# Depthwise convolution of a transformer block's feed-forward part: one run of 32x32 array tiles over four banks in place of two runs of 64x64 tiles

## The reference, cut to what matters

```python
def bit_linear(x, w):                 # values: round(x * 127 / max|x| per row), weights: -1, 0, 1 and a scale
    return jnp.einsum('bsd,hd->bsh', xq, wq)

h = bit_linear(x, w1)                 # 16 x 128 x 256 -> 16 x 128 x 1024
h = depthwise_conv1d(h.transpose(0, 2, 1), conv_w, conv_b)   # 3 taps along the 128 rows, each of the 1024 units by itself
h = jax.nn.silu(h.transpose(0, 2, 1))
return bit_linear(h, w2)              # -> 16 x 128 x 256
```

## Time and profile before

| what | value |
|---|---|
| runs | 995.89, 996.27, 1000.37 us; median 996.27 us |
| profiled execution, first to last instruction (its span) | 992.7 us |
| its mean granted TensorE clock | 0.962 of 2.4 GHz |
| PE busy over the span | 891.3 us (90%) |
| feed-forward part | about 876 to 992.7 us of the span |
| PE instructions of CV in the trace | 1536 matmul records, 1536 weight loads |

### The profile page before, as it was taken

One profiled execution on the slowest core, in us unless ns is written; L12 is line 12 of the kernel. 1 busy time (PEld: TensorE's weight loads), 2 busy tenths in 40 slices (PEclk: granted clock), 3 DMA queues, 4 the chain that ended last, 5 costly groups with the idle time before them and its releaser, 6 DMA issues. The chain is left out here.

```text
span 992.7 us, 26217 instructions
## 1 busy us (share of the span) xinstructions
PE 891.3 (90%) x8784; PEld 758.1 (76%) x8785; DVE 612.0 (62%) x1561; ACT 469.1 (47%) x1209; POOL 379.8 (38%) x555
## 2 busy tenths in 40 slices
PE   4888889777999999997999899999999999779995
PEld 3677667636999999995556598888888887667784
DVE  3588788754455555542017466768667686549895
ACT  3777777712222222221333444445444454349895
POOL 4477677530000000006101446445464444426762
PEclk9998999987999999998999999999999999879998
DMA  4454447432433333315765798897989986411121
GB/s 119 145 164 145 143 148 237 140 145 94 128 108 93 98 93 108 93 44 181 262 225 180 165 188 185 179 182 164 200 172 176 172 178 150 90 33 55 60 61 49
DMA packets 222059, 137.78 MB, mean 139 GB/s; under 512 B 160289, under 2 KB 207393, under 8 KB 221857
## 3 DMA queue, kind: packets, MB, share of 16 engines
q1 hardware_dynamic: 180304, 99.78, 40.1%
q10 hardware_dynamic: 38608, 28.64, 10.8%
q0 software_dynamic: 3072, 8.39, 2.6%
HBM read 81.79 MB, written 54.98 MB: 138 GB/s over the span
## 5 line engine op out<-in xcount | busy, mean ns | idle before, releaser
L1717 ACT ACTIVATE c_pT<-c_T 128x512 f32<-128x512 f32 (+2 forms) x90 | 50.2, 595 | 104.4 <-PE c_T L1876 73.3
L1666 POOL TENSOR_TENSOR c_soft<-c_soft,c_share 128x616 f32<-128x616 f32 (+2 forms) x96 | 70.3, 760 | 63.4 <-DVE c_share L2129 61.8
L1062 ACT ACTIVATE b_rowsT<-b_RT 128x256 f32<-128x256 f32 x39 | 15.0, 383 | 158.2 <-PE b_RT L1104 158.2
L1173 DVE COPY b_w<-moe_w 128x1024 f32 x78 | 53.5, 687 | 56.2 <-issue 50.7
L1676 POOL MEMSET d_round<- 128x1 f32 x1 | 0.1, 98 | 226.5 <-POOLq L953 226.5
L1113 PEld LDWEIGHTS b_G<-b_rowsT,b_w 128*128 128x128 f32 x624 | 77.2, 195 | 4.2 <-DVE b_w L1173 1.5
L1113 PE MATMUL b_G<-b_rowsT,b_w 128*128 128x128 f32 x624 | 77.9, 279 | 1.5 <-ACT b_rowsT L1062 1.3
L1113 PE MATMUL b_U<-b_rowsT,b_w 128*128 128x128 f32 x624 | 76.1, 275 | 0.0
L1187 DVE SCALAR_TENSOR_TENSOR b_hidT<-b_U,b_bias,b_gate 128x128 f32<-128x128 f32 x156 | 43.9, 343 | 51.9 <-PE b_U L1113 45.4
L1140 PE MATMUL b_Y<-moe_w,b_hidT 128*128 x312 | 73.9, 380 | 0.9 <-DVE b_out L1218 0.9
L1113 PEld LDWEIGHTS b_U<-b_rowsT,b_w 128*128 128x128 f32 x624 | 72.9, 192 | 0.0
(11 more groups left out here) (231 smaller groups left out, 2167.2 us busy)
## 6 DMA issues: line engine op xcount, KB each, us to landing
rel_windows<-c_relw ACTq DMA_DIRECT2D x28, 368.0 KB, 6.7
c_bias<-rel_windows SPq DMA_DIRECT2D x16, 616.0 KB, 5.6
prob_rows<-c_soft SPq DMA_DIRECT2D x16, 616.0 KB, 7.3
moe_w<-in_L_Wl SPq DMA_DIRECT2D x16, 512.0 KB, 4.1
early<-in_L_early SPq DMA_DIRECT2D x16, 384.0 KB, 3.2
values<-c_pT ACTq DMA_DIRECT2D x22, 256.0 KB, 3.8
b_rows<-expert_lists SPq DMA_DIRECT2D x39, 128.0 KB, 2.0
expert_out<-b_out SPq DMA_DIRECT2D x39, 128.0 KB, 1.7
```

The source lines that it names most:

```text
L1173: nc.vector.tensor_copy(own[p][h][:, :, :], w1[:, bass.ds(e, 1), :, h * HE:(h + 1) * HE].rearrange("p o c n -> p (o c) n"))\
L1666: ins = nc.gpsimd.tensor_tensor(soft[p][:, hs, a:z], soft[p][:, hs, a:z], share[:, s, hs].unsqueeze(2).to_broadcast([P, HS, z - a]), ALU.mult)
L1717: nc.scalar.activation(dst, view(T[k]), ACT.Copy, **kw).then_inc(g["emptied"], 1)
```

## The change

The 16 blocks' work of a batch becomes one run, `convolve(b, p)`: 96 matmuls, each on one 32x32 tile. Blocks 0 to 3 go with the first three taps' turns, blocks 4 to 7 with the second; for each tap 16 matmuls follow each other on the 16 tiles. Row quarter `a` of the array writes to bank `CV[a]`, block `m` = half * 4 + turn puts its quarter `a` into quarter (a + turn) % 4 of the output's partitions, and the host permutes the second weight matrix and the biases to suit (`turned_quarters`). The run waits once, for `d_hp`(b+1) and for all eight SiLUs of the batch before, and raises `cv_mm` once; all eight SiLUs of a batch wait for that. The list of PE loses its second call. POOL's tap matrices are 128x32 in place of 128x64.

```diff
-    c["halves"] = np.concatenate([np.eye(P // 2, dtype=np.float32)] * 2)
+    c["quarters"] = np.concatenate([np.eye(P // 4, dtype=np.float32)] * 4)
...
-                    nc.gpsimd.tensor_scalar(shared["tap"][:, m, k, :], cst("halves"), taps[:, m, k:k + 1], None, ALU.mult)
+                    nc.gpsimd.tensor_scalar(shared["tap"][:, m, k, :], cst("quarters"), taps[:, m, k:k + 1], None, ALU.mult)
...
         def tiles_of(half):
-            return [(half * 2 + u + cross * MH // 2, cross, CV[half * 2 + cross][:, u * P:(u + 1) * P]) for u in two for cross in two]
+            return [(half * 4 + r, CV[r][:, half * P:(half + 1) * P]) for r in range(4)]
...
-                act.wait_ge(g["cv_mm"], 2 * b + half + 1)
+                act.wait_ge(g["cv_mm"], b + 1)
                 since(act, g["rounded"], b - 1)
-                for m, _, region in tiles_of(half):
+                for m, region in tiles_of(half):
...
-            def convolve(b, p, half):
-
-                if half == 0:
-                    pe.wait_ge(g["h"], b + 1)
-                apart(pe, g["silu"], 2 * (b - 1) + half + 1)
-                tiles = tiles_of(half)
-                for u, k in itertools.product(two, range(3)):
-                    for m, cross, region in tiles[2 * u:2 * u + 2]:
-                        for a in two:
-                            r, c = a * HALF, (a ^ cross) * HALF
-                            ins = nc.tensor.matmul(region[c:c + HALF, :], tap[r:r + HALF, m, k, :], hp[p][r:r + HALF, m, k:k + P],
+            def convolve(b, p):
+
+                pe.wait_ge(g["h"], b + 1)
+                apart(pe, g["silu"], 2 * b)
+                for half, k in itertools.product(two, range(3)):
+                    tiles = tiles_of(half)
+                    for turn in range(4):
+                        m = half * 4 + turn
+                        for a in range(4):
+                            r, c = a * QUART, (a + turn) % 4 * QUART
+                            ins = nc.tensor.matmul(tiles[a][1][c:c + QUART, :], tap[r:r + QUART, m, k, :], hp[p][r:r + QUART, m, k:k + P],
                                                    start=(k == 0), stop=(k == 2), tile_position=(r, c))
                 ins.then_inc(g["cv_mm"], 1)
...
             def steps(b, i, p):
                 if there(b + 1):
-                    convolve(b + 1, 1 - p, 0)
+                    convolve(b + 1, 1 - p)
                 if there(b + 2):
                     hidden(b + 2)
                 if there(b):
                     highest(b)
-                if there(b + 1):
-                    convolve(b + 1, 1 - p, 1)
...
-                since(dve, g["cv_mm"], 2 * (b - 1))
+                since(dve, g["cv_mm"], b - 1)
...
-def crossed_halves(a):
-
-    a = a.reshape(2, MH // 2, 2, HALF, -1)
-    return np.stack([a[0], a[1][:, ::-1]]).reshape(HID, -1)
+def turned_quarters(a):
+
+    a = a.reshape(2, 4, 4, QUART, -1)
+    return np.stack([[[a[h, (c - r) % 4, r] for c in range(4)] for r in range(4)] for h in range(2)]).reshape(HID, -1)
```

More of the change, by code:

```diff
@@ L1230 @@
 HALF = P // 2
+QUART = P // 4
 FLOOR = 1e-5
@@ L2605, in build @@
         shared["ffn"] = [sb(f"ffn_w{k}", [P, W_N // P], BF16)[:, :] for k in range(2)]
-        shared["tap"] = sb("ffn_tap", [P, MH, 3, HALF])
+        shared["tap"] = sb("ffn_tap", [P, MH, 3, QUART])
         shared["ffn_unit"] = sb("ffn_unit", [P, 2])
@@ L2633, in layout1 @@
         "L1_alphas": np.stack([L1_xattn_alpha, L1_xattn_beta]),
-        "L1_w1T": L1_ffn_w1.T, "L1_w2T": crossed_halves(L1_ffn_w2.T), "L1_conv_w": L1_ffn_conv_w.reshape(HID, 3),
-        "L1_conv_b": crossed_halves(L1_ffn_conv_b).reshape(MH, P).T,
+        "L1_w1T": L1_ffn_w1.T, "L1_w2T": turned_quarters(L1_ffn_w2.T), "L1_conv_w": L1_ffn_conv_w.reshape(HID, 3),
+        "L1_conv_b": turned_quarters(L1_ffn_conv_b).reshape(MH, P).T,
     }
```

## The result

| | before | after |
|---|---|---|
| median of the runs | 996.62 us | 1038.86 us |
| ratio, 95% interval | | 1.042 [1.039, 1.045] |
| profiled execution, its span | 992.7 us | 1032.5 us |
| its mean granted clock | 0.962 | 0.959 |
| first `d_gi` to last `d_gi` | 897.95 to 986.57 | 909.51 to 1026.32 |

What follows compares the result with a forecast made beforehand. Bound: the ring, 6.05 us a step. Terms +1.2, +0.7 and -0.9 made +1.0 us, span 992.7 to 993.7; with the median 3.6 us above, 997.3 us, own range 995 to 1001, 8 in 10 from 993 to 1013.

Steps and rivals of the forecast that it cites:

- The ring: Chain from one d_gi to the next through Y, CV, H, d_hp, d_peak, unit, inverse: 6.05 us a step, no slack.
- step 1: Convolution's second half leaves its place between top and the transposes; it was covered by DVE's work, so gain 0.
- Step 2: Whole batch's convolution replaces the first half in the ring: 1.6 us from start to H against 1.48, +1.2 us in all.
- lower bound: Whole convolution run to H if each tile keeps its 12 records and pace, all tiles side by side: about 1.55 us.
- upper bound: Whole convolution run if no more records start per microsecond than before: 5.2 us by their distance.
- Rival A2: Convolution run has only eight or so tiles at once: 1.9 to 2.8 us, up to 1015 us in all; chance 0.14.
- Step 3: Convolution run waits for all eight SiLUs of the batch before: 0.3 us to spare, so 0.
- Step 4: SiLUs wait for the whole convolution run: 0 in the steady part, up to a CV of 2.1 us.
- Step 5: At the start, the second batch's run waits for the first batch's last SiLUs: 1.0 us lost, +0.7 us in all.
- Step 6: At the end, the last four SiLUs follow the first four directly, without waiting for CV: -0.9 us in all.
- Rival B: PE's sum is the bound, then DVE or ACT takes over: 0.33 us on 10 intervals, about 992 us; chance 0.13.
- Rival C: Clock falls as PE idles more each step: ring grows some 2.5 us, about 1030 us; chance 0.04.

Runs made afterwards that it cites:

- second_one_tap: Kernel before with the middle tap alone in the convolution's second half: 995.08 us, 1.000 of the kernel before.
- hidden_first: Changed kernel with H(b+2) put ahead of the convolution's run, nothing else moved: 1027.89 us, 1.032 of the kernel before.
- bf16_twice: Changed kernel in bf16 with each product made twice, again 384 instructions a batch: 1030.07 us, 1.030 of the kernel before.
- quarter_columns: Changed kernel with 32 of the 128 columns of each convolution matmul, same number of instructions: 1027.32 us.
- experiment 12: Changed kernel with its code moved by 80 instructions, 20 float32 matmuls ahead of PE's first feed-forward work: 1037.95 us.
- eight_tiles: Changed kernel with the run's 96 matmuls reordered, eight tiles at a time with their three taps, then the next eight: 1038.33 us.
- half_columns: Changed kernel with 64 of the 128 columns of each convolution matmul, same number of instructions: 1031.15 us.
- after_unrolled: Changed kernel with its hardware loop unrolled: 1039.11 us, 1.044 of the kernel before.
- split_columns: Changed kernel with its run cut in two, blocks 4 to 7 behind the turn of top, semaphore raised once after the second: 1026.16 us, 1.033 of the kernel before.
- shifted: The kernel of experiment 12, the changed kernel with 80 instructions put ahead of PE's first feed-forward work: 1037.95 us.
- one_tap: Changed kernel with the middle tap alone, 128 instructions a batch in place of 384: 1000.01 us, 1.001 of the kernel before.
- bf16_quarters: Changed kernel (32x32 tiles) with taps and d_hp in bf16 in place of float32: 997.89 us, 1.001 of the kernel before.
- bf16_halves: Kernel before (64x64 tiles) with taps and d_hp in bf16 in place of float32: 995.23 us, 0.995 of the kernel before.
- bf16_unrolled: bf16_halves with its hardware loop unrolled: 990.50 us, 0.996 of the kernel before.
- bf16_second_twice: bf16_halves with the convolution's second half made twice to keep PE busy: 991.20 us, 0.996 of the kernel before.

## Why the prediction was wrong, step by step

- *The ring*, *step 1* (the second half is covered) and the place of the run: right. PE waits 1.82 us for `d_unit` where the half was; `second_one_tap` and `hidden_first` bear it out.
- *Step 2* failed: the whole run was priced at 1.6 us from CV to H and took 2.67. I took the lower bound, each tile's own work, because "every row for a part of the array is at that end". Those rows have at most four tiles side by side. The records of 16 tiles are held by two more things: a pace of one record (a weight load and a matmul) each 8.3 ns past the first 32, 1.6 us for 192, as `bf16_twice` and `quarter_columns` show (1.73 and 1.77 to H); and for float32 with 128 columns another 0.9 us that falls with the columns. The latter I can't explain: by the tiles' own work alone (12 records of 0.109 us) it should be hidden. It stays open.
- The *upper bound* of step 2, 5.2 us by the old distance of records, was far off. The 25 ns that the Trainium skill ("TensorE: Matmul & The Clock Gate", "Wait — 56ns, not 53.3ns?") puts between starts is contradicted for different tiles: 32 starts within 0.24 us (a timeline of the kernel after cut at 953.71 shows x32 begun at 953.47).
- *Rival A2* had the right size: a run of 2.8 us, 1015 us in all. With the run alone, some 13 us by the sum above, the kernel would be near that; no run shows it. I gave it 0.14, and cut my range just under it. Its mechanism, only eight tiles at once, is neither shown nor excluded: it gives the 13.6 ns a record of `eight_tiles` and nearly the 14 of the kernel after, but with 64 columns (6.8 ns by half the tiles' work, an estimate) the 8.3 ns pace should hold, and `half_columns` took 1.9 us from first to last record, about 10 ns each.
- **No step and no rival had the pauses.** In the kernel after they are some 12 of the 39.8 us, with the reserve of experiment 12. I counted the change's 48 more matmuls a batch as time on the array and as issue, never as code: of 64 bytes an instruction, 24 KB a batch in place of 12. The rows to ask were on the page: queue q8, 44 packets of instructions, hidden then. `after_unrolled`, `split_columns`, `bf16_twice` and `shifted` show each a side of it. The Trainium skill ("Runtime: NRT & Kernel Launch", "Instruction fetch mechanics") says that crossing a 16 KiB boundary is mostly hidden. The trace agrees for the kernel before; in a run this dense the boundary cost 0.7 to 2.0 us where it brought a pause.
- *Step 3* right: in the loop the run starts behind Y without a wait for a SiLU. *Step 4*: given for up to 2.1 us, so void at 2.67; ACT's SiLUs waited 22.2 us for CV, though in the loop the ring and not this set the step.
- *Step 5* had the wait right: the second run starts behind the last SiLU of batch 0, PE idle for 2.29 us. From first run to second 2.2 us were added, 1.3 by the longer first run and 0.9 by this wait (I had said 1.0). Its +0.7 in all can't be read off, under 11.6 us of longer runs, pauses and low clock. *Step 6* half right: the eight SiLUs of the last batch follow each other, and `d_act` starts 2.37 us after the first of them in place of 3.01. It was given back:

```profile
1016.29 2.18 ACT L2356 ACTIVATE d_act<-d_CV,d_cbias 128x128 f32<-128x128 f32 x8 [2.67 <-PE d_CV L2430]
...
1022.80 1.89 PE L2450 MATMUL d_Y<-ffn_w,d_gi 128*128 128x256 bf16 x8
...
1025.10 1.20 ACT L2367 ACTIVATE d_whole<-d_act,d_round 128x1024 f32<-128x1024 f32 x1
```

  After an end with more idle PE the clock fell one product earlier, Y took 1.89 us for 1.05, and ACT's last rounding stands behind it in its list.
- *Rival B*: DVE's list binds at 5.9 us, so the most that a free ring could give was 0.15 us a step, not 0.33. *Rival C*: a low clock cost some microseconds at the start and one run; the mean hardly moved (0.959 for 0.962).

## What to carry to other kernels

Cutting a product into more and smaller array tiles multiplies the instructions, and float32 doubles them again; price them as supply (8.3 ns a record here once 32 have been used up) and as code, since each 256 are a fetch of 16 KB that took 2.3 to 2.7 us from its start to the first instruction behind it. A dense run on the critical ring pays both, a hidden one less, and a hardware loop pays the fetch in its first pass alone. Look at the instruction queue of the DMA view before adding instructions; and before shortening an engine's list ask which list is next, from its steps and not from its busy share.

## What the runs showed of the hardware that I had not expected

- Records on different tiles start up to 32 in 0.24 us, then one each 8.3 to 8.5 ns (bf16, or float32 of 32 columns), 14 ns on average for float32 of 128 columns (2.74 less a record's 0.27 and 0.24, over 160).
- A fetch of PE's code is invisible at 96 instructions in 1.5 us and can be a pause with 384 in a run; where the pause comes, it stays behind the same instruction (record 189 at 2.7 us a run as at 1.8) and moves with the code.
- Less work on PE is not always a gain: in `one_tap`, `bf16_quarters` and `bf16_halves`, with PE busy 53 to 54 of 75 us, the granted clock fell to 0.84 to 0.89, and steps with a stretch at the 1.2 GHz level were 6.8 to 7.1 us in `one_tap` in place of 5.9, which took away what the shorter run had gained. With the same busy time, 53.0, 53.4 and 54.2 us, the clock was 0.95 in the kernel after, `bf16_unrolled` and `bf16_second_twice`. What decides it stays open.
